# The first part of a four-layer graph network kernel in another order: own rows' sums and U ahead, two scalings on ScalarE

## The chip, the cores and the metric

The kernel runs on one core of a Trainium2 chip. The metric is the device time of one execution in microseconds (us); lower is better. The engines are TensorE (PE; its weight loads are PEld), VectorE (DVE), ScalarE (ACT), GpSimd (POOL) and SyncE (SP, which here only issues DMAs). Each runs its own list of instructions in order, and semaphores tie the lists together.

## The reference, cut to what matters

Sixteen graphs of 512 nodes with 128 features go through four layers, each followed by a layer norm:

```python
x = _layernorm(x + _L0_gnn_ref(x, adj, ...))   # adj @ (x @ W) + bias
x = _layernorm(x + _L1_gnn_ref(x, adj, ...))   # 5 groups of the first 25 nodes, two graph convolutions each
x = _layernorm(x + _L2_gnn_ref(x, adj, ...))   # mask * exp(e_i + f_j), rows normalised, times h
x = _layernorm(x + _L3_gnn_ref(x, adj, ...))   # conv 17 taps, gaussian message passing, GRU cell
```

Layer 1 touches the first 25 nodes of a graph alone. For each group it takes the block of the adjacency that the group's mask leaves, adds the identity, and scales it on both sides by the inverse root of its row sums:

```python
A = adj + jnp.eye(n)
deg = jnp.sum(A, axis=-1)
norm_adj = dinv[:, :, None] * A * dinv[:, None, :]     # dinv = deg ** -0.5
support = jnp.einsum('bnd,de->bne', x, W)
out = jax.nn.relu(jnp.einsum('bnm,bme->bne', norm_adj, support) + b)
```

## The kernel before

The program has two parts with a barrier of all engines between them. The second part is a software pipeline over the sixteen graphs. It starts at 72.83 us, and the change leaves it as it is. The first part prepares all that the pipeline needs: graph 0 through layers 0 to 2, layer 1 of the other fifteen graphs at once, and the weights.

The fifteen graphs are packed as `PT` = 3 tiles of `PJ` = 5 graphs with 25 nodes each, so `R` = 125 rows. What the first part does for them, by the names in the code:

- `mask_blocks(t)` (DVE) makes the masked blocks `A5[t]` of 5 groups and their row sums `deg`. `inverse_degrees` turns the sums into inverse roots with a power that POOL computes (`degree_root`). The blocks are scaled by rows (L730), `block_rows(t)` (PE) transposes them into PSUM, and `scale_columns(t)` (DVE, L596) scales the other side into `nadjT`.
- `own_sums(q)` (PE, L888) computes layer 0 for the first 25 nodes of each graph ("own rows"), four graphs at a time. It needs the x tiles `xt[0..2]`, which SP loads one after the other. ACT copies the sums (`copy_natural`), PE transposes them (`transpose_sums`), ACT copies them again (`copy_sums`), and `own_outputs` (L903) multiplies by the weight. DVE adds x (L791), takes statistics (L795, L799) and normalises (L810) to `x1P`; the semaphore is `q_nP`.
- The products U = `x1P` times `nadjT` (L1056, L1057) follow, then `hidden(gi)`, `second_layer(gi)` and `mix_nodes(gi)` for the five groups. Between them stand `transpose_second(mc)`, which turns the adjacency of graph 1, and `transpose_weights(k)`, which turns the weights of layer 3. ACT rounds the turned weights (`round_weights`), DVE keeps the rest (`rest_of_weights`).

Beside that runs graph 0: its hidden products (L993), second layer (L1009) and mix (L1015), DVE's masked outputs (L747), their sum (L752), statistics, x2, a dot product that gives `ef` (L632), ACT's exponential `pef` (L528), and the split of x2 times `pef` into `x_hi` (ACT, L531) and `x_lo` (DVE, L787). The second aggregate (L264 to L266: twelve passes of 512 columns into bank 5) uses them, and `OUT2` (L1048) is the product of that aggregate with layer 2's weight.

The order of each engine is written out by hand, and the PSUM banks are given by hand too (`W_BANK`, `TT_BANK`). SP's list waits at two places: the load of the 17 taps (`nat_c2`, L383) waits for `own_sums(1)`, since it overwrites `xt[0]`, and the load of the adjacency of graph 1 is behind it.

## Time and profile before

| | us |
| --- | --- |
| median of 3 runs | 576.24 |
| lowest, highest | 575.03, 576.47 |
| the profiled execution, its device time | 576.53 |
| the profiled execution, its span | 574.8 |
| PE busy | 552.4 |
| DVE busy | 481.9 |
| ACT busy | 393.2 |
| POOL busy | 218.1 |

Times in the trace count from the start of the span. A timeline row gives the start, the length, the engine, the line, the operation with its operands, how many instructions were merged (x), and in brackets how long the engine stood idle just before and what released it. One fp32 product on PE appears as two matmuls in the trace, so x10 there is five in the code. A merged row's length runs from the start of its first to the end of its last instruction.

### The profile page before, as it was taken

To read this page: it belongs to the slowest core of one execution; us is meant where nothing else is said; L and a number is where in the kernel's file an instruction comes from. 1 tells how busy PE (TensorE), PEld (TensorE's weight loads), DVE (VectorE), ACT (ScalarE), POOL (GpSimd) and SP (SyncE) were. 2 spreads that over 40 slices of the span, in tenths; PEclk is the share of its full clock that TensorE was granted. 3 is DMA by queue.
4 is the path that set the end of the run, shared out by engine and by line. 5 is a ranking of instruction groups with operands and counts; after the bars stand their busy time and mean duration, and the time that the engine had idled before them with its cause. 6 is when DMAs were issued, how large, how long until landed. Compare 5 with 4: busy or idle time off the path is not lost.

```text
span 574.8 us, 12128 instructions
## 1 busy us (share of the span) xinstructions
PE 552.4 (96%) x3639; PEld 487.4 (85%) x3639; DVE 481.9 (84%) x1768; ACT 393.2 (68%) x828; POOL 218.1 (38%) x213
## 2 busy tenths in 40 slices
PE   5879999999999999999999999999999999999994
PEld 5767988888989898989889898989898888989684
DVE  3897868889898988888888989888888889898665
ACT  2425666777786867777678778687677777786452
POOL 3311134353444435263534435353525353443010
PEclk9998999999999999999999999999999999999998
DMA  7890041003030303020020303030302103000000
GB/s 183 261 328 13 2 133 68 2 14 100 1 111 0 110 0 110 0 88 23 24 86 0 110 0 110 0 110 0 110 0 58 52 10 101 2 19 19 1 21 18
DMA packets 33301, 34.46 MB, mean 60 GB/s; under 512 B 1663, under 2 KB 22531, under 8 KB 33146
## 3 DMA queue, kind: packets, MB, share of 16 engines
q1 hardware_dynamic: 32986, 34.01, 18.7%
q8 instruction: 13, 0.21, 0.2%
q10 hardware_dynamic: 288, 0.13, 0.1%
q14 instruction: 14, 0.11, 0.1%
HBM read 29.74 MB, written 4.39 MB: 59 GB/s over the span
## 4 chain that ended last, share of the span: by engine, by line
PE 85%; DVE 1%; ACT 1%; issue 0%; POOLq 0%; POOL 0%; DVEq 0%
PE bank L264 14%; PE bank L266 14%; PE bank L265 14%; PE pair L264 6%; PE pair L266 6%; PE pair L265 6%; PE bank L1665 5%; PE bank L1676 3%; PE bank L1769 2%; PE pair L1825 2%; PE pair L1757 2%; PE bank L1860 2%; PE bank L1861 2%; PE bank L1864 2%; PE bank L1730 1%; PE bank L1840 1%
## 5 line engine op out<-in xcount | busy, mean ns | idle before, releaser
L1153 POOL TENSOR_TENSOR rs<-ve,neg_half 128x4 f32<-128x4 f32 (+1 forms) x60 | 54.8, 913 | 134.9 <-DVE ve L1389 100.9
L1187 POOL TENSOR_TENSOR P_lo<-P,P_hi 128x512 fp32r<-128x512 f32 x56 | 81.9, 1482 | 50.7 <-ACT P_hi L1226 50.7
L264 PE MATMUL bank<-cd_hi,w_hi 128*128 128x256 f32 x272 | 77.1, 284 | 0.0
L265 PE MATMUL bank<-cd_lo,w_hi 128*128 128x256 f32 x272 | 76.5, 281 | 0.0
L266 PE MATMUL bank<-cd_hi,w_lo 128*128 128x256 f32 x272 | 76.2, 280 | 0.0
L1424 DVE TENSOR_TENSOR P<-bank,aT 128x512 f32<-128x512 f32 x64 | 41.1, 684 | 18.5 <-ACT bank L1212 18.4
L264 PE MATMUL pair<-aT_hi,x_hi 128*128 128x512 f32 x128 | 53.3, 416 | 1.4 <-DVE x_lo L787 1.4
L265 PEld LDWEIGHTS bank<-cd_lo,w_hi 128*128 128x128 f32 x272 | 51.2, 188 | 1.6
L264 PEld LDWEIGHTS bank<-cd_hi,w_hi 128*128 128x128 f32 x272 | 51.3, 189 | 1.4
L266 PEld LDWEIGHTS bank<-cd_hi,w_lo 128*128 128x128 f32 x272 | 51.4, 189 | 0.0
L266 PE MATMUL pair<-aT_hi,x_lo 128*128 128x512 f32 x128 | 51.0, 398 | 0.0
L265 PE MATMUL pair<-aT_lo,x_hi 128*128 128x512 f32 x128 | 50.7, 396 | 0.0
L1226 ACT ACTIVATE P_hi<-P 128x512 fp32r<-128x512 f32 x56 | 32.2, 630 | 17.9 <-DVE P L1424 17.9
L1408 DVE TENSOR_TENSOR aT_lo<-bank,aT_hi 128x512 fp32r<-128x512 f32 x56 | 38.5, 687 | 6.9 <-ACT aT L1208 6.9
L1163 POOL TENSOR_TENSOR x<-x_nat,bias 128x512 f32<-128x512 f32 x15 | 19.7, 1314 | 64.1 <-DVE x3T_lo L1494 64.1
L264 PE MATMUL bank<-co_hi,w_hi 128*128 128x256 f32 x144 | 41.8, 290 | 0.2 <-DVE co_lo L1511 0.2
L266 PE MATMUL bank<-co_hi,w_lo 128*128 128x256 f32 x144 | 40.7, 282 | 0.0
L265 PE MATMUL bank<-co_lo,w_hi 128*128 128x256 f32 x144 | 40.5, 281 | 0.0
L1208 ACT ACTIVATE aT<-bank 128x512 f32<-128x512 f32 x56 | 34.8, 621 | 0.0
L1212 ACT ACTIVATE bank<-bank 128x512 f32<-128x512 f32 x64 | 34.4, 575 | 0.0
L1206 ACT ACTIVATE aT_hi<-bank 128x512 fp32r<-128x512 f32 x56 | 34.3, 613 | 0.0
L1345 ACT ACTIVATE nmp_hi<-bank 128x512 fp32r<-128x512 f32 x16 | 9.6, 600 | 35.8 <-PE bank L1864 32.2
(378 smaller groups left out, 1696.1 us busy)
## 6 DMA issues: line engine op xcount, KB each, us to landing
adj_nat<-in_adj_dram SPq DMA_DIRECT2D x16, 1024.0 KB, 5.9
x_nat<-in_x_dram SPq DMA_DIRECT2D x16, 256.0 KB, 2.9
xt<-in_x_dram SPq DMA_DIRECT2D x3, 1280.0 KB, 11.1
out_dram<-y_out SPq DMA_DIRECT2D x15, 256.0 KB, 2.3
hw<-in_L_gnn_W_dram SPq DMA_DIRECT2D x2, 640.0 KB, 6.5
xt<-in_L_gnn_conv_w_dram SPq DMA_DIRECT2D x1, 1088.0 KB, 6.9
aT<-in_adj_dram SPq DMA_DIRECT2D x5, 96.0 KB
nat_ih<-in_L_gnn_w_ih_dram SPq DMA_DIRECT2D x1, 384.0 KB, 5.7
```

Of the source, the lines that this page charges most:

```text
L264: nc.tensor.matmul(o, lh, rh, start=start, stop=False)
L265: nc.tensor.matmul(o, lh, rl, start=False, stop=False)
L266: return nc.tensor.matmul(o, ll, rh, start=False, stop=stop)
L1153: g.tensor_tensor(rs[i][:, 0:n], ve[i][:, 0:n], neg_half[:, 0:n], ALU.pow).then_inc(po_rs[i], 1)
L1187: g.tensor_tensor(P_lo[:, mc, :], P[:, mc, :], f(P_hi[:, mc, :]), ALU.subtract).then_inc(po_Plo[mc], 1)
L1206: s.activation(aT_hi[:, mc, :], AT_OF[mc][:, :], ACT.Identity)
L1208: s.activation(aT[par][:, mc, :], AT_OF[mc][:, :], ACT.Identity).then_inc(ac_aT[mc], 1)
L1212: s.activation(AT_BANK[mc % 2][:, :], AT_BANK[mc % 2][:, :], ACT.Exp, scale=2.0).then_inc(ac_E[mc], 1)
L1226: s.activation(P_hi[:, mc, :], P[:, mc, :], ACT.Identity).then_inc(ac_Phi[mc], 1)
L1408: v.tensor_tensor(aT_lo[:, mc, :], AT_OF[mc][:, :], f(aT_hi[:, mc, :]), ALU.subtract).then_inc(dv_aTlo[mc], 1)
L1424: v.tensor_tensor(P[:, mc, :], AT_BANK[mc % 2][:, :], aT[par][:, mc, :], ALU.mult).then_inc(dv_P[mc], 1)
L1665: last = t_.transpose(AT_OF[mc][:, ch(c)], adj_nat[par][:, c, ch(mc)], ident[:, :])
```

## The change

The work stays the same, apart from three moves between engines or banks; the rest is order.

- The scaling of the masked blocks by rows (L730, three DVE instructions of 125x625) becomes `scale_rows(t)`: five ACT instructions of 125x125 for each tile. DVE's `inverse_degrees` for it moves ahead of `c12`.
- The scaling of the 17 taps (L842, one DVE instruction of 128x2176) becomes one ACT instruction in `scale_taps`, ahead of ACT's copy of the second aggregate.
- `transpose_sums` writes bank 5 in place of bank 0, and two weight groups change banks.
- On PE `block_rows(1)` goes ahead of graph 0's mix, the sums of all own rows go ahead of the blocks of tiles 2 and 3, `transpose_sums` goes ahead of the first weights, `transpose_weights(1)` and the products U go ahead of `OUT2`, and `transpose_second(0)` goes behind `hidden(0)`.
- On DVE `scale_columns` of tiles 1 and 2 goes behind graph 0's statistics, the sum and the statistics of the own rows go ahead of the split `x_lo`, and the rests of two weight groups move.
- On POOL the sum of tap pairs goes ahead of graph 0's last inverse root and waits for `dv_e`.

SP's list is unchanged. The diff, cut:

```diff
-        W_BANK = [bank[i] for i in (4, 4, 1, 6, 5, 0, 1, 6, 5, 0)]
-        NAT_BANK, TT_BANK = bank[4], bank[0]
+        W_BANK = [bank[i] for i in (4, 6, 0, 6, 5, 0, 1, 6, 5, 0)]
+        NAT_BANK, TT_BANK = bank[4], bank[5]
...
+                def scale_rows(t):
+                    for gi in range(NG):
+                        last = s.activation(A5[0:R, t, gi, :], A5[0:R, t, gi, :], ACT.Identity,
+                                            scale=deg[0:R, 3, NG * t + gi:NG * t + gi + 1])
+                    last.then_inc(q_B, 1)
...
+                act.wait_ge(q_dgi, 2)
+                scale_rows(1)
                 act.wait_ge(q_S0, 1)
...
+                scale_rows(2)
+                scale_rows(3)
                 copy_natural()
+                copy_sums()
                 round_weights(-1)
-                copy_sums()
...
+                round_weights(0)
+                round_weights(1)
+                scale_taps()
+                act.wait_ge(pe_agg2, 1)
+                s.activation(agg_sb[:, :], AG_BANK[:, :], ACT.Identity).then_inc(ac_agg2, 1)
                 for t in range(PT):
                     copy_u(t)
+                act.wait_ge(dv_e, 1)
+                s.activation(pef[:, 0, :], ef[:, 0, :], ACT.Exp, bias=c12[:, 0:1]).then_inc(ac_pe, 1)
+                relu_hidden(0)
                 split_second(0)
-                relu_hidden(0)
                 split_second(1)
...
                 v.tensor_scalar(hT0[:, :, :], hT0[:, :, :], 0.0, None, ALU.max).then_inc(q_own, 2)
+                inverse_degrees(R, NG, NT * NG, 2)
                 dve.wait_ge(q_vsb, 1)
...
-                inverse_degrees(R, NG, NT * NG, 2)
-                for t in range(1, NT):
-                    v.tensor_tensor(A5[0:R, t], A5[0:R, t], spread(deg[0:R, 3, NG * t:NG * (t + 1)], R), ALU.mult).then_inc(q_B, 1)
...
-                v.tensor_scalar(nat_c2, nat_c2, bn_scale[:, 1:2], None, ALU.mult).then_inc(q_sc2, 1)
...
+                block_rows(1)
                 pe.wait_ge(q_c12, 1)
                 pe.wait_ge(q_S0s, 1)
...
-                block_rows(1)
                 own_sums(1)
-                block_rows(2)
-                block_rows(3)
                 own_sums(2)
                 own_sums(3)
+                block_rows(2)
                 pe.wait_ge(q_sumsb, 1)
+                transpose_sums()
                 pe.wait_ge(q_sc1, 1)
                 transpose_weights(-1)
-                transpose_sums()
+                block_rows(3)
...
+                pe.wait_ge(q_whi, 1)
                 pe.wait_ge(q_nP, 5)
                 pe.wait_ge(q_nT, NT + 1)
                 for t in range(PT):
...
+                pe.wait_ge(ac_agg2, 1)
+                pe.wait_ge(q_unit, 1)
+                pe.wait_ge(q_wlo, 1)
+                for c in range(NC):
+                    last = t_.matmul(OUT2[:, c // 2, c % 2, :], agg_sb[:, ch(c)], wwT, start=True, stop=True)
+                last.then_inc(pe_out2, 1)
                 hidden(0)
+                pe.wait_ge(adj_in[1], 16)
                 pe.wait_ge(q_wlo, 2)
+                transpose_second(0)
                 transpose_second(1)
```

DVE at the degrees and the row scaling; hT is graph 0's hidden layer, c its two constants, hb the second bias. Before:

```order
L709 TENSOR_SCALAR hT<-hT 128x250
L711 COPY c<-bank 128x2
...
L724 TENSOR_REDUCE hsum<-hb 125x128
L727 TENSOR_TENSOR fused_in<-x,hsum 25x128
L577 TENSOR_TENSOR deg<-deg 125x15
L730 TENSOR_TENSOR A<-A,deg 125x625 x3
L632 ISA prod,ef<-x,v 128x128
```

And now:

```order
L725 TENSOR_SCALAR hT<-hT 128x250
L593 TENSOR_TENSOR deg<-deg 125x15
L728 COPY c<-bank 128x2
...
L741 TENSOR_REDUCE hsum<-hb 125x128
L744 TENSOR_TENSOR fused_in<-x,hsum 25x128
L648 ISA prod,ef<-x,v 128x128
```

The inverse degrees (deg 125x15) come eight rows earlier, behind hT, and the three scalings of 125x625 are gone; the products for `ef` (ISA rows) follow `fused_in` directly.

DVE ahead of the second aggregate; bank in L791 (now L798) is the own rows' product. Before:

```order
L747 SCALAR_TENSOR_TENSOR prod<-pair,wm,hb 25x128
L596 TENSOR_TENSOR nadjT<-bank,deg 125x500
L752 TENSOR_REDUCE red<-prod 25x128
...
L777 TENSOR_SCALAR x<-x,mv,rs 128x128
L632 ISA prod,ef<-x,v 128x128
L632 ISA ef 128x1
L782 CAST x_hi<-pef 128x4
L784 TENSOR_TENSOR x_lo<-pef,x_hi 128x4
L787 SCALAR_TENSOR_TENSOR x_lo<-x,pef,x_hi 128x127 x4
L791 TENSOR_TENSOR x1P<-bank,xP 125x384
```

And now:

```order
L761 SCALAR_TENSOR_TENSOR prod<-pair,wm,hb 25x128
L765 TENSOR_REDUCE red<-prod 25x128
...
L775 TENSOR_SCALAR ve<-mv 128x1
L612 TENSOR_TENSOR nadjT<-bank,deg 125x500 x2
...
L648 ISA prod,ef<-x,v 128x128
L648 ISA ef 128x1
L798 TENSOR_TENSOR x1P<-bank,xP 125x384
L802 BN_STATS stP<-x1P 125x6 x3
L805 CAST x_hi<-pef 128x4
L807 TENSOR_TENSOR x_lo<-pef,x_hi 128x4
L810 SCALAR_TENSOR_TENSOR x_lo<-x,pef,x_hi 128x127 x4
```

One scaled tile of columns no longer stands ahead of the sum `red`, two stand behind the statistics, and the own rows' sum and statistics stand ahead of the cast and the split `x_lo`.

PE from the last passes of the second aggregate to the second layer. Before:

```order
L266 MATMUL pair<-aT_hi,x_lo 128x512
L946 MATMUL bank<-ident,adj_nat 128x128 x4
L1048 MATMUL pair<-plainT,agg_sb 128x130 x4
L939 MATMUL bank<-ident,nat_ih 128x128 x4
L1056 MATMUL bank<-nadjT,x1P 128x125
L1057 MATMUL bank<-nadjT,x1P 128x300
...
L916 MATMUL bank<-A,hw 128x375 x2
L946 MATMUL bank<-ident,adj_nat 128x128 x4
L925 MATMUL bank<-hw,aPT 125x128 x6
```

And now:

```order
L266 MATMUL pair<-aT_hi,x_lo 128x512
L1056 MATMUL bank<-nadjT,x1P 128x125
L1057 MATMUL bank<-nadjT,x1P 128x300
...
L1064 MATMUL pair<-plainT,agg_sb 128x130 x4
L925 MATMUL bank<-A,hw 128x375 x2
L955 MATMUL bank<-ident,adj_nat 128x128 x8
L934 MATMUL bank<-hw,aPT 125x128 x6
```

U (nadjT, x1P) follows the aggregate directly, `OUT2` (plainT, agg_sb) comes behind it, and all eight transposes of graph 1's adjacency stand behind the hidden products.

## Rows read from the trace of the kernel before

**Rows 1.** Stretches of the span: us, busy by engine (instructions), PEclk, DMA share, GB/s

```profile
38.00:43.00 5.00, 2.49 (x18) 2.11 (x19) 3.81 (x20) 2.82 (x11) 1.15 (x2) 0.96 0.98 359
43.00:48.00 5.00, 4.75 (x17) 3.57 (x17) 4.69 (x16) 1.16 (x3) 0.85 (x1) 0.70 0.10 36
...
73.00:574.00 501.00, 493.54 (x3144) 435.36 (x3142) 427.84 (x1558) 362.38 (x760) 201.96 (x179) 1.00 0.14 46
```

**Rows 2.** Timeline, DVE, 28 to 48 us: start, us, engine, line, operation [idle before]

```profile
28.27 0.16 DVE L711 COPY c<-bank 128x2 f32<-128x2 f32 x1
...
31.75 2.25 DVE L730 TENSOR_TENSOR A<-A,deg 125x625 f32<-125x625 f32 x3
...
35.27 1.11 DVE L747 SCALAR_TENSOR_TENSOR prod<-bank,wm,hb 25x128 f32<-25x128 f32 x4
...
36.56 0.66 DVE L596 TENSOR_TENSOR nadjT<-bank,deg 125x500 f32<-125x500 f32 x1
...
41.08 0.29 DVE L632 CUSTOM_DVE_ANT_0 prod<-x,v 128x128 f32<-128x128 f32 x1
...
42.31 1.23 DVE L787 SCALAR_TENSOR_TENSOR x_lo<-x,pef,x_hi 128x127 fp32r<-128x127 f32 x4
43.45 0.55 DVE L791 TENSOR_TENSOR x1P<-bank,xP 125x384 f32<-125x384 f32 x1
44.11 0.68 DVE L795 BATCH_NORM_STATS2 stP<-x1P 125x6 f32<-125x128 f32 x3
...
47.61 0.85 DVE L810 TENSOR_SCALAR x1P<-x1P,mvP,rsP 125x128 f32<-125x128 f32 x3
```

**Rows 3.** Timeline, POOL, first 74 us

```profile
26.25 2.76 POOL L423 TENSOR_TENSOR deg<-deg,neg_half 125x15 f32<-125x15 f32 x1 [2.76 <-DVE deg L571]
...
37.60 0.99 POOL L432 TENSOR_TENSOR xP<-xP,bias 125x384 f32<-125x384 f32 x1 [7.93 <-DMA xP<-in_x_dram]
...
59.28 1.90 POOL L441 TENSOR_TENSOR xt<-xt 128x1024 f32<-128x1024 f32 x1 [2.56 <-DVE xt L842]
```

**Rows 4.** Timeline, ACT, first 74 us

```profile
21.37 1.57 ACT L512 ACTIVATE aT<-bank 128x512 f32<-128x512 f32 x3
...
41.81 1.27 ACT L531 ACTIVATE x_hi<-x,pef 128x127 fp32r<-128x127 f32 x4
```

**Rows 5.** Timeline, PE, 31 to 73 us

```profile
31.57 1.03 PE L1015 MATMUL bank<-prod,nadjT 25*25 25x128 f32 x8 [0.93 <-ACT prod L523]
...
35.78 1.95 PE L888 MATMUL bank<-xt,aPT 128*32 128x128 f32 x56
...
42.81 0.77 PE L264 MATMUL pair<-aT_hi,x_hi 128*128 128x512 f32 x1 [1.36 <-DVE x_lo L787]
...
46.90 0.39 PE L266 MATMUL pair<-aT_hi,x_lo 128*128 128x512 f32 x1
...
49.41 0.38 PE L1056 MATMUL bank<-nadjT,x1P 125*128 125x125 f32 x2
...
54.73 1.55 PE L925 MATMUL bank<-hw,aPT 128*125 128x128 f32 x12 [0.32 <-ACT aPT L475]
...
57.03 0.82 PE L934 MATMUL bank<-S,nadjT 125*125 125x128 f32 x6
...
72.83 0.63 PE L1730 MATMUL bank<-ident,x 128*128 128x128 f32 x4 [1.25 <-PEq L1086]
```

**Rows 6.** Loads of the x tiles, by tile: count, shortest/median/longest issue ns, first and last start

```profile
L350 SPq DMA_DIRECT2D xt<-in_x_dram x3: 389/889/4240, 11.6 to 21.3; - x3
```

**Rows 7.** DMA issues: the x tile issued last, in its own stretch; then the taps' load

```profile
xt<-in_x_dram SPq DMA_DIRECT2D x1, 1280.0 KB, 14.1
...
xt<-in_L_gnn_conv_w_dram SPq DMA_DIRECT2D x1, 1088.0 KB, 6.9
```

**Rows 8.** Timeline, DVE, 57 to 62 us

```profile
57.86 1.34 DVE L842 TENSOR_SCALAR xt<-xt,bn_scale 128x2176 f32<-128x2176 f32 x1
...
60.36 1.23 DVE L612 TENSOR_TENSOR fusedP<-R,hsum 125x384 f32<-125x384 f32 x1
```

More of the change, by code:

```diff
@@ L436, in _ @@
                 g.tensor_tensor(rsP[0:R, :], veP[0:R, :], neg_half[0:R, 0:PT], ALU.pow).then_inc(q_rsP, 1)
-                pool.wait_ge(dv_ve[2], 1)
-                g.tensor_tensor(rs[2][:, :], ve[2][:, :], neg_half[:, 0:NC], ALU.pow).then_inc(po_rs[2], 1)
+                pool.wait_ge(dv_e, 1)
                 pool.wait_ge(q_sc2, 1)
@@ L441, in _ @@
                 g.tensor_tensor(nat_sum, nat_c2[:, :, 0:TAPS - 1:2], nat_c2[:, :, 1:TAPS:2], ALU.add).then_inc(q_sum, 1)
+                pool.wait_ge(dv_ve[2], 1)
+                g.tensor_tensor(rs[2][:, :], ve[2][:, :], neg_half[:, 0:NC], ALU.pow).then_inc(po_rs[2], 1)
             @block.scalar
@@ L531, in _, with scale_taps @@
                     s.activation(x_hi[:, c, 1:D], x2[:, c, 1:D], ACT.Identity, scale=pef[:, 1, c:c + 1]).then_inc(ac_xs[c], 1)
-                round_weights(0)
-                act.wait_ge(pe_agg2, 1)
-                s.activation(agg_sb[:, :], AG_BANK[:, :], ACT.Identity).then_inc(ac_agg2, 1)
-                act.wait_ge(dv_e, 1)
-                s.activation(pef[:, 0, :], ef[:, 0, :], ACT.Exp, bias=c12[:, 0:1]).then_inc(ac_pe, 1)
-                round_weights(1)
+                def scale_taps():
+                    act.wait_ge(q_bns, 2)
+                    act.wait_ge(q_wc2, 16)
+                    s.activation(nat_c2, nat_c2, ACT.Identity, scale=bn_scale[:, 1:2]).then_inc(q_sc2, 1)
                 def split_second(mc):
@@ L749, in _ @@
                 last.then_inc(q_own, 1)
-                scale_columns(1)
                 dve.wait_ge(q_own, 5)
@@ L762, in _ @@
                 v.tensor_scalar(ve[1][:, 0:1], mv[1][:, 0, 1:2], EPS, None, ALU.add).then_inc(dv_ve[1], 1)
+                scale_columns(1)
+                scale_columns(2)
                 dve.wait_ge(q_bnr, 1)
@@ L780, in _ @@
                 dot(1, 0).then_inc(dv_f, 1)
+                dve.wait_ge(q_o, 1)
+                dve.wait_ge(q_xPb, 1)
+                v.tensor_tensor(x1P[0:R, :, :], bank[7][0:R, 0:PT * D].rearrange("p (t d) -> p t d", t=PT), xP[0:R, :, :],
+                                ALU.add).then_inc(q_nP, 1)
+                hold(dve, q_nP, 1)
+                for t in range(PT):
+                    last = v.bn_stats(stP[0:R, t, :], x1P[0:R, t, :])
+                last.then_inc(q_nP, 1)
                 hold(dve, ac_pf, 1)
@@ L788, in _ @@
                                            ALU.mult, ALU.subtract).then_inc(dv_xs[c], 1)
-                dve.wait_ge(q_o, 1)
-                dve.wait_ge(q_xPb, 1)
-                v.tensor_tensor(x1P[0:R, :, :], bank[7][0:R, 0:PT * D].rearrange("p (t d) -> p t d", t=PT), xP[0:R, :, :],
-                                ALU.add).then_inc(q_nP, 1)
-                hold(dve, q_nP, 1)
-                for t in range(PT):
-                    last = v.bn_stats(stP[0:R, t, :], x1P[0:R, t, :])
-                last.then_inc(q_nP, 1)
                 hold(dve, q_nP, 2)
@@ L802, in _ @@
                 v.tensor_scalar(veP[0:R, :], mvP[0:R, :, 1], EPS, None, ALU.add).then_inc(q_nP, 1)
-                scale_columns(2)
                 scale_columns(3)
@@ L815, in _ @@
                 last.then_inc(dv_e, 1)
+                rest_of_weights(0)
+                rest_of_weights(1)
                 hold(dve, pe_out2, 1)
@@ L828, in _ @@
                 last.then_inc(dv_y3, 1)
-                rest_of_weights(1)
                 rest_of_second(0)
@@ L1034, in _ @@
                 transpose_weights(0)
+                pe.wait_ge(q_nT, 2)
+                transpose_weights(1)
                 pe.wait_ge(dv_pf, 1)
@@ L1041, in _ @@
                 last.then_inc(pe_agg2, 1)
-                pe.wait_ge(adj_in[1], 16)
-                pe.wait_ge(q_TTs, 1)
-                transpose_second(0)
-                pe.wait_ge(ac_agg2, 1)
-                pe.wait_ge(q_unit, 1)
-                for c in range(NC):
-                    last = t_.matmul(OUT2[:, c // 2, c % 2, :], agg_sb[:, ch(c)], wwT, start=True, stop=True)
-                last.then_inc(pe_out2, 1)
-                pe.wait_ge(q_nT, 3)
-                transpose_weights(1)
-                pe.wait_ge(q_wlo, 1)
+                pe.wait_ge(q_whi, 1)
                 pe.wait_ge(q_nP, 5)
```

6 lines of the change are left out of this document (removed).

## The prediction

> **What bounds the kernel now.** I read the stretches first, then each engine's timeline of the first 73 us. Behind 73 us PE is busy 493.54 of 501 us at full clock [rows 1], and the change leaves that code alone. So the question is when the second part starts; it does at 72.83 us [rows 5]. Before that PE is busy 2.49 of the 5 us from 38 to 43 [rows 1]. There it waits for a chain over DVE, POOL and ACT: graph 0's outputs, sum, statistics and `ef`, then the split `x_lo`, which the second aggregate waits for until 42.81 [rows 5]. PE's granted clock fell behind that thin stretch: it is 0.70 in the mean of 43 to 48 us [rows 1], which is 3.0 us at the lower level (1.2 GHz) and the rest at 2.4 GHz. The U products wait for PE's own order until 49.41 [rows 5]. From the second layer on (54.73) PE runs nearly without gaps to the barrier. Below, steps of 0.65 us or less without a group are the small instructions and hand-overs of the same timelines, moved with their own lengths.
>
> **Step 1, the degrees, a wait added on DVE.** POOL's power ends at 29.01 [rows 3]. `inverse_degrees` used to come long after it; now DVE reaches it at 28.2, since its next row starts at 28.27 [rows 2]. DVE waits some 0.8 us, and with the operation itself and its hand-over `c12` starts at 29.25, 0.98 late. All of DVE is queued behind. In return the three scalings (31.75, 2.25 us) and the old place of the degrees leave, 33.92 - 31.57 = 2.35 us. Graph 0's outputs (L747) start at 35.27 + 0.98 - 2.35 = 33.90, 1.37 earlier.
>
> **Step 2, the scalings on ACT.** Four scaled activations of 127 columns take 1.27 us [rows 4], 0.3 us from start to start, so five take 1.6: 29.25 to 30.8. ACT's copy of graph 0's S0 waits behind them; PE's second layer ended at 30.64 (31.57 less the 0.93 idle [rows 5]), so the copy loses some 0.1. `block_rows(1)` fits into the wait that stood there, and the mix starts at about 31.55 as before and ends near 32.7, which is ahead of DVE at 33.90: no cost. Tiles 2 and 3 take 3 us on ACT, 31.4 to 34.4, ahead of a copy that isn't due before 37.4: no cost, by the cover of the loads.
>
> The Trainium skill's page "ScalarE: Activation LUTs" (What ACT_TABLE_LOAD costs) gives 280 ns and 0.833 ns a column for an activation with a pointer operand. By it the scaled 125 columns take 0.38 us, and the trace agrees (its x_hi rows are 0.38 to 0.40 long, 1.27 for four that overlap); the taps of 2176 columns would take 2.1 us by that estimate, and the sum below would not change.
>
> **Step 3, the own rows' sums.** The third x tile is issued at 21.3 [rows 6] and lands 14.1 us later [rows 7], at 35.4. PE reaches the sums that need it at about 33.75 and waits 1.7 us. The sums used to start at 35.78 and last 1.95 [rows 5], so they end at 37.4, only 0.35 earlier: the loads hold this branch. Then `block_rows(2)` (0.65) covers ACT's copy, the transposed sums, first weights and `block_rows(3)` cover the second copy, and `own_outputs` ends at 40.3.
>
> **Step 4, graph 0's statistics.** The sum of the outputs no longer has `scale_columns(1)` ahead of it (0.58 of the 0.66 in the row is its own step [rows 2]), so the statistics are 1.37 + 0.58 = 1.95 earlier, at 37.65. Two scalings of columns (1.17) follow, so the bn rows, x2 and the dot product come 0.78 earlier: 41.08 becomes 40.30 [rows 2]. POOL's inverse root stands behind the x sum that ends at 38.59 [rows 3]; with 0.56 it is done at 39.2, under DVE's scalings.
>
> **Step 5, the own rows ahead of the split.** DVE now does the sum and the statistics (0.55 and 0.68 [rows 2], 1.27 with the hand-over) between the dot product and the cast, where 0.43 us of waiting for ACT stood. That eats the 0.78: the cast comes at 41.87, `x_lo` starts at 42.37 for 42.31 before, and the aggregate at 42.87 for 42.81. The term is zero, from -0.8 (were it hidden) to +0.8 (were `own_outputs` late by that much).
>
> **Step 6, the clock.** Where PE was thin before, it now has all its transposes and weights: busy from 35.45 to 41.2 almost without a gap, idle 33.75 to 35.45 and 41.2 to 42.87. I take it that the clock stays up. The twelve passes took 42.81 to 46.90 from first to last start [rows 5]; 3.0 us at the lower level are 1.5 at the upper, so it is 2.6 now. The aggregate ends at 45.8 instead of 47.2. The range is 0 to 1.5.
>
> **Step 7, U.** DVE still needs after `x_lo` (1.2): aggregation and variance (0.5), one scaling of columns (0.6) and the last (0.46), then, with POOL's root under them, the normalisation (0.85 [rows 2]): 43.5 to 46.0. Before, 1.23 of sum and statistics, one more scaling and a weights' rest stood between as well. U starts at 46.1 for 49.41, 3.3 earlier, bound by DVE and no longer by PE. ACT's taps scaling (between the DVE's 1.34 [rows 8] and, by four times the width of a 0.49 us copy [rows 4], 2.1) runs 43.3 to 45.4, ahead of the copy of the aggregate due at 45.9: hidden, by 0.5 us; if it is late, `OUT2` is, behind U's 2.2 us of cover.
>
> **Step 8, to the second layer.** U ends at 48.3, `OUT2` (1.0) at 49.3, `hidden(0)` (1.3) at 50.6, eight transposes (0.9) at 51.5. Beside them `y3` is done at 51.4 and the relu at 51.4. The second layer starts at 51.5 for 54.73: 3.2 earlier. Now ACT is late: two split pairs and x_hi, five copies of 0.5 [rows 4], run 51.4 to 53.9 ahead of `copy_s2(0)`. So the first `mix_nodes` starts at 54.4 for 57.03 [rows 5], 2.6 earlier; 0.5 is given back.
>
> **Step 9, the tail.** From there PE has the same list as before and I let it keep its pace. DVE is later against PE than before, by up to 1 us, but has lost the taps (1.34). On POOL the tap pairs leave the tail. There `fusedP` (60.36) took 1.23 us while POOL's 1.90 us sum ran [rows 3, 8]. The Trainium skill's page "SBUF — State Buffer" (Who interferes with whom) says that a DVE instruction with two SBUF inputs contends with a GpSimd instruction that reads SBUF. By that rule and this row the tail loses a stall of some 0.6 on DVE. At the new place DVE's weight rests read one operand from PSUM, and by the same rule they don't stall. Without it the rivals below hold as they are, with a thinner margin.
>
> **The sum.** Against the profiled execution (span 574.8, device time 576.53): -2.6 at the barrier, plus 0.2 that I add for new hand-overs between engines, is -2.4, so 574.1. That execution lies 0.3 over the median of the three runs (576.24), for which I forecast 573.8.
>
> **The rivals.**
> A, the clock falls again. PE has 1.7 us of idle twice, the second just ahead of the aggregate; for the fall speaks that before it fell behind 2.5 busy us in 5, against it that PE is now busy some six in nine. Then the aggregate ends at 47.2 and U starts there: 1.1 less gain, 574.9.
> B, the tail becomes DVE's and ACT's. The third mix needs DVE's second group added by 61.9 and my replay has it at 61.85; if DVE's chain from the late `aT_lo` (52.4 for 53.40, only 1.0 earlier) sets the end, the gain is between 1.0 and 1.6: 575.0. Against it, PE is ahead of DVE's need by 0.6 or more at all later places.
> C, slower: the x rows of POOL's sum land later. That wait ended at 37.60 [rows 3], and the taps' load (1088 KB, 6.9 us [rows 7]) is issued 0.8 earlier, since `own_sums(1)` ends earlier. At 359 GB/s [rows 1] it is 3.0 us of traffic. If it goes ahead of those rows, POOL's sum ends at 41.6, the root at 42.2, the dot at 42.8, and with step 5's 1.3 in front the aggregate starts at 45.3 at the lower clock, U at 49.65, the first mix at 57.9 for 57.03: 577.1, and 578 with one more half us at any wait. It turns into a loss when the rows land more than 2.3 us late. Against it: they were issued before the taps.
> D, more gain: ACT's backlog of step 8 is hidden and no hand-over costs: -3.2, 573.0.
>
> **How the numbers follow.** Forecast 0.54, A 0.2, B 0.13, C 0.06, D 0.07. The bound of what a measurement tells apart is 0.3%, 1.7 us: faster means below 574.5. The forecast is faster in nine cases of ten, D always, A and B in one of five: 0.62. C gives slower in two of three: 0.04. The rest, 0.34, is the same. The range goes from 572.8 (D) to 575.8 (A or B with 0.8 to spare).
>
> **What would show it.** The first steps: DVE idle 0.8 ahead of the degrees, L761 (graph 0's outputs) near 33.9, PE idle until 35.4 ahead of the sums. Then the cast near 41.9, the aggregate's passes at 0.39 and not 0.77, U at 46.1, the second layer at 51.5, the first mix with 0.5 of wait for ACT, and the second part's first row (72.83 before) at 70.4. Passes at 0.77 mean A; idle on PE ahead of L943 behind the first mix means B; POOL's sum later than 37.6 means C.

## The result, and the profile after

| | before | changed |
| --- | --- | --- |
| median, us | 575.19 | 574.25 |
| lowest to highest | 573.91 to 578.61 | 572.86 to 575.77 |
| runs | 19 | 19 |
| the profiled execution, device time | 576.53 | 573.76 |
| its span | 574.8 | 572.0 |

The ratio is 0.9969, 95% interval 0.9954 to 0.9983: the change takes 0.31% off, 0.9 us at the medians, where the forecast took off 2.4. The two profiled executions lie 2.8 us apart. Most of this text is about that difference.

PE's timeline of the changed kernel, 32 to 70 us, answers [rows 5]:

```profile
32.53 1.08 PE L898 MATMUL bank<-xt,aPT 128*32 128x128 f32 x32
35.05 1.95 PE L898 MATMUL bank<-xt,aPT 128*32 128x128 f32 x56 [1.44 <-DMA xt<-in_x_dram]
...
42.35 0.47 PE L264 MATMUL pair<-aT_hi,x_hi 128*128 128x512 f32 x1 [1.42 <-DVE x_lo L810]
...
44.94 0.39 PE L266 MATMUL pair<-aT_hi,x_lo 128*128 128x512 f32 x1
45.87 0.46 PE L1056 MATMUL bank<-nadjT,x1P 125*128 125x125 f32 x2 [0.54 <-issue]
...
51.35 1.58 PE L934 MATMUL bank<-hw,aPT 128*125 128x128 f32 x12
...
54.02 0.92 PE L943 MATMUL bank<-S,nadjT 125*125 125x128 f32 x6 [0.17 <-ACT S L490]
...
69.92 0.63 PE L1738 MATMUL bank<-ident,x 128*128 128x128 f32 x4 [1.25 <-PEq L1094]
```

The aggregate starts 0.46 us earlier than in [rows 5], and its twelve passes take 2.59 us from first to last start, where they took 4.09. U starts 0.93 behind the start of the last pass. The second part starts at 69.92 for 72.83, and from there to the end it is 502.1 us for 502.0: nothing changed behind the barrier.

The stretches of the changed kernel, for the first two of [rows 1]:

```profile
38.00:43.00 5.00, 3.58 (x29) 3.25 (x29) 4.62 (x23) 3.27 (x11) 0.63 (x2) 1.00 0.88 308
43.00:48.00 5.00, 4.46 (x23) 3.38 (x22) 4.33 (x19) 3.57 (x5) 2.16 (x2) 1.00 0.08 31
```

PE is busy 3.58 of the 5 us ahead of the aggregate, and the granted clock is 1.00 in both stretches.

DVE of the changed kernel, 28 to 46 us, answers [rows 2]:

```profile
28.77 0.17 DVE L593 TENSOR_TENSOR deg<-deg 125x15 f32<-125x15 f32 x1 [0.91 <-POOL deg L423]
...
33.60 1.11 DVE L761 SCALAR_TENSOR_TENSOR prod<-bank,wm,hb 25x128 f32<-25x128 f32 x4
...
40.12 0.29 DVE L648 CUSTOM_DVE_ANT_0 prod<-x,v 128x128 f32<-128x128 f32 x1
40.34 0.08 DVE L648 DVE_READ_ACCUMULATOR2_ANT ef<- 128x1 f32 x1
40.34 0.55 DVE L798 TENSOR_TENSOR x1P<-bank,xP 125x384 f32<-125x384 f32 x1
40.99 0.68 DVE L802 BATCH_NORM_STATS2 stP<-x1P 125x6 f32<-125x128 f32 x3
41.59 0.15 DVE L805 CAST x_hi<-pef 128x4 fp32r<-128x4 f32 x1
...
44.90 0.86 DVE L823 TENSOR_SCALAR x1P<-x1P,mvP,rsP 125x128 f32<-125x128 f32 x3 [0.38 <-issue]
```

DVE waits 0.91 us for the degrees, and the own rows' sum and statistics stand between the dot product and the cast without a gap. The scaled `x1P`, which U needs, is 2.71 us earlier than in [rows 2].

ACT and then DVE's tail of the changed kernel; they answer [rows 4] and [rows 8]:

```profile
28.98 1.56 ACT L468 ACTIVATE A<-A,deg 125x125 f32<-125x125 f32 x5 [1.09 <-DVE deg L593]
...
42.98 2.11 ACT L546 ACTIVATE xt<-xt,bn_scale 128x2176 f32<-128x2176 f32 x1
45.36 0.60 ACT L556 ACTIVATE agg_sb<-pair 128x512 f32<-128x512 f32 x1 [0.28 <-PE pair L266]
```

```profile
57.84 0.56 DVE L628 TENSOR_TENSOR fusedP<-R,hsum 125x384 f32<-125x384 f32 x1
```

### The profile page after: what moved, and what is told of

The parts are those of the page before. It is cut to its first block, busy times and chain, and to the rows that moved or that the text cites. A ratio compares the mean times of both kernels' runs of the same rounds, so it can differ in the third digit from the quotient of the medians.

```text
span 572.0 us, 12140 instructions
## 1 busy us (share of the span) xinstructions
PE 552.4 (97%) x3639; PEld 488.0 (85%) x3639; DVE 479.0 (84%) x1764; ACT 398.9 (70%) x844; POOL 218.7 (38%) x213
## 4 chain that ended last, share of the span: by engine, by line
PE 85%; DVE 1%; ACT 1%; issue 0%; POOLq 0%; POOL 0%; DVEq 0%
PE bank L264 14%; PE bank L266 14%; PE bank L265 14%; PE pair L264 6%; PE pair L266 6%; PE pair L265 6%; PE bank L1673 5%; PE bank L1684 3%; PE bank L1777 2%; PE pair L1833 2%; PE pair L1765 2%; PE bank L1868 2%; PE bank L1869 2%; PE bank L1872 2%; PE bank L1738 1%; PE bank L1848 1%
## 5 line engine op out<-in xcount | busy, mean ns | idle before, releaser
L266 PEld LDWEIGHTS bank<-cd_hi,w_lo 128*128 128x128 f32 x272 | 51.5, 189 | 0.0
```

Of the source, the lines that this page charges most:

```text
L266: return nc.tensor.matmul(o, ll, rh, start=False, stop=stop)
```

## The experiments

The runs are told in the order of the questions. In the tables, "clock low" is where the granted clock of a trace stood at its lower level (1.2 GHz) in the first 73 us, from stretches of 1 us; elsewhere it was 2.4 GHz. "Adjacency" is the start of PE's transposes of graph 0's adjacency (L968, before L959), which wait for its load.

### Is the first trace typical? Both kernels again

**The changed kernel, unchanged.**

> The changed kernel unchanged, timed beside the kernel before on the same chip, for its spread. Its trace starts the second part 2.9 us earlier (69.92 for 72.83), yet the medians of 19 runs each differ by 0.9 us. Theory 1 (the clock varies by execution): the fall ahead of the second aggregate happens in some executions of either kernel, so the mean granted clock differs from run to run and goes with the time; ratio to before 0.996 to 0.998. Theory 2 (the order alone): every execution gains the 2.6 to 2.9 us of the traces; ratio 0.9950 to 0.9955.

Measured: 574.5 us, ratio 0.9976 (0.996 to 0.9992). Its profiled execution took 576.44, as long as the one of before. PE in it:

```profile
44.42 0.77 PE L264 MATMUL pair<-aT_hi,x_hi 128*128 128x512 f32 x1 [1.42 <-DVE x_lo L810]
44.98 0.63 PE L265 MATMUL pair<-aT_lo,x_hi 128*128 128x512 f32 x1
...
48.66 0.38 PE L1056 MATMUL bank<-nadjT,x1P 125*128 125x125 f32 x2
```

The passes are 0.63 long: the clock is low in the aggregate of the changed kernel too, with the same instructions and the same 1.42 us of wait ahead of it as in the first trace. So the clock that stayed up in the first trace does not belong to its program.

**The kernel before, twice more**, and the changed kernel a third time.

> The kernel before, unchanged, for a second trace of it. Theory (the clock falls at places that differ from one execution to the next): the granted clock is at its lower level somewhere else than at 42.6 to 46 us; if it stays up through the aggregate, the aggregate's passes take 0.39 us each, OUT2 follows 1.4 us earlier than 47.98, and the second part starts at 71.0 to 71.8 instead of 72.83, counted from the same landing of the adjacency (11.6). Rival (the fall in the aggregate belongs to this program): low at 42 to 46 again, the aggregate's passes 0.63 us, the second part at 72.5 to 73.2. Both: 501.9 to 502.1 us from the start of the second part to the end.

> The kernel before, unchanged, for a third trace of it, to see what its stretch from the aggregate to the second part takes where the clock is up in the aggregate: in both traces so far the clock is low there (30.02 and 30.13 us), in the kernel before with idle transposes it is up (28.55, with U held by nothing of DVE's). Theory (about 1.0 to 1.5 us of the distance between the two first traces is this fall, which comes in some executions only): if the rows show the clock up from 42 to 47 us, 28.5 to 29.1 from the aggregate's start to the second part's, so that against the changed kernel's 27.57 there are 1.0 to 1.5 left, as the medians say; if it is low there again, 29.9 to 30.2, and the question is left to the medians. Rival (the kernel before is slow there for another reason, DVE's order): 29.5 or more with the clock up.

> The changed kernel, unchanged, for a third trace. Theory: the low stretches are at other places again; between the adjacency's landing and U there are 34.5 us where the clock stays up in between (34.55 in the first trace of it) and 37 to 37.6 where a stretch lies in the first layer as well as in the aggregate (37.6 in the second trace). The start of the second part is 24.0 to 24.1 us behind U in either case. Rival (the first trace is what this kernel does, the second was a disturbance): 34.5 us again and the lower level at 11.8 to 15.1 alone.

Measured, one execution each: 577.9, 573.86 and 574.79 us. Of the second of these, the kernel before with its granted clock up throughout, this is PE; the last rows are 40 to 70 us:

```profile
19.38 0.48 PE L980 MATMUL bank<-ident,vrows 28*128 28x128 f32 x2 [1.23 <-DMA vrows<-in_L_gnn_b_dram]
...
40.92 0.47 PE L264 MATMUL pair<-aT_hi,x_hi 128*128 128x512 f32 x1 [1.33 <-DVE x_lo L787]
...
43.49 0.39 PE L266 MATMUL pair<-aT_hi,x_lo 128*128 128x512 f32 x1
...
45.57 0.60 PE L939 MATMUL bank<-ident,nat_ih 128*128 128x128 f32 x4
46.67 0.46 PE L1056 MATMUL bank<-nadjT,x1P 125*128 125x125 f32 x2 [0.50 <-issue]
...
52.06 1.55 PE L925 MATMUL bank<-hw,aPT 128*125 128x128 f32 x12 [0.32 <-ACT aPT L475]
...
54.37 0.82 PE L934 MATMUL bank<-S,nadjT 125*125 125x128 f32 x6
...
70.17 0.63 PE L1730 MATMUL bank<-ident,x 128*128 128x128 f32 x4 [1.25 <-PEq L1086]
```

The stretches of the same execution:

```profile
38.00:43.00 5.00, 3.41 (x19) 2.92 (x20) 3.99 (x20) 2.16 (x7) 0.42 (x1) 1.00 0.71 252
43.00:48.00 5.00, 4.25 (x28) 3.37 (x28) 4.46 (x20) 1.15 (x3) 0.85 (x1) 1.00 0.01 2
```

All traces of the two kernels, and one of the changed kernel with its degrees later (below), in us:

| kernel | clock low | adjacency | to the aggregate | from there to U | from the aggregate to the second part | adjacency to second part |
| --- | --- | --- | --- | --- | --- | --- |
| before, first | 12 to 15, 42 to 46 | 11.61 | 31.20 | 6.60 | 30.02 | 61.22 |
| before, second | 20 to 31, 44 to 48 | 10.58 | 33.58 | 6.71 | 30.13 | 63.71 |
| before, third | nowhere | 10.09 | 30.83 | 5.75 | 29.25 | 60.08 |
| changed, first | 12 to 15 | 11.32 | 31.03 | 3.52 | 27.57 | 58.60 |
| changed, second | 20 to 31, 44 to 48 | 11.04 | 33.38 | 4.24 | 28.23 | 61.61 |
| changed, third | 20 to 28 | 10.99 | 32.06 | 3.51 | 27.57 | 59.63 |
| degrees later | nowhere | 11.51 | 31.07 | 3.51 | 27.57 | 58.64 |

Like with like, counted from the adjacency: with the clock up everywhere the changed order is worth 60.08 - 58.64 = 1.4 us; with the low stretches at the same two places (the two second traces) 2.1; in the first pair, where only before's aggregate was slow, 2.6. The second trace of before had its aggregate slow again, so it spoke for the rival there; the third decides it, since the same program ran its aggregate at 0.39 us a pass. Its 29.25 lies between what was expected, 28.5 to 29.1, and the 29.5 or more of the rival that named DVE's order, and both have a part in it: with the clock up U waits until DVE's `x1P` is ready (46.57; it starts at 46.67). The third trace of the changed kernel has a low stretch at a third place, ahead of the aggregate only, and U comes 35.6 us behind the adjacency, between the two figures that were expected; the second part follows U by 24.06. The clock is not all of that: graph 0's outputs start where they did in the first trace (33.62 for 33.60), and what then comes late is the third x tile (36.02 for 35.05), behind which PE turns the blocks that DVE waits for. Two other sources of spread are as large as the effect: a trace with a low stretch at 20 to 31 us is 2.3 us (33.38 for 31.07, changed order) to 2.8 (33.58 for 30.83, before) longer up to the aggregate, and the adjacency lands anywhere from 10.1 to 11.6.

The 1.4 us has a weak part and a firm one. Ahead of the aggregate PE waits for loads that don't follow the adjacency at a fixed distance: 1.23 us for `vrows` in the third trace of before (above), 0.47 in the run with the degrees later. Counted from the start of the trace, the second parts of these two start at the same time, 70.17 and 70.15. Behind the aggregate no load is waited for, and there every trace of the changed kernel is ahead of every trace of before, by 1.68 us where the clock is up in both (29.25 and 27.57) and by 1.9 where it is low in both (30.13 and 28.23).

Over all timed runs, single executions left out, the kernel before takes 575.70 in the mean of 104 runs (spread 1.3), the changed one 574.42 in 31 (spread 0.9): 1.3 us less, 95% interval 0.9 to 1.7 from these spreads. By the clock, where it is on record: the runs whose mean granted clock over the span is 0.995 or more have means of 574.4 (before, 17 runs) and 573.6 (changed, 8); those from 0.987 to under 0.991, 576.6 (25) and 574.7 (11). By these means the change is worth 0.7 us where the clock hardly fell and 1.9 where it did.

### Can idle products hold the clock up?

```diff
+                def keep_busy(n):
+                    for i in range(n):
+                        t_.transpose(bank[5][:, 0:D], ident[:, :], ident[:, :])
...
+                keep_busy(11)
```

In the changed kernel `keep_busy(11)` stands ahead of `own_sums(2)` and ahead of the aggregate. The second kernel is the kernel before with 5, 4 and 11 of them in its three gaps.

> The changed kernel with eleven idle transposes of the identity into bank 5 in each of PE's two gaps (ahead of the sums that wait for the third x tile, and ahead of the second aggregate). They add no work that anyone waits for. If the clock falls in these gaps in some executions (theory 1), the median drops by up to 0.5 us and the spread shrinks. If it never falls there (theory 2), the time is that of the changed kernel within 0.2 us.

> The kernel before with idle transposes into bank 5 in its three gaps between 37.7 and 42.8 us (five, four and eleven). If the fall of the clock cost it time (theory 1), the second aggregate's passes are 0.39 us long and no longer 0.77, the aggregate ends 1.4 us earlier, and U starts at 48.5 for 49.41, since DVE's normalisation ends only then: 0.9 us less at the start of the second part, and up to 0.9 in the median. If the clock was not what held U (theory 2: DVE's chain did), the time is that of before within 0.2.

Measured: 574.08 us, ratio 0.9971 (0.9953 to 0.9989), no different from the changed kernel; and 576.41, ratio 1.0012 (0.9992 to 1.0032), no faster than before. In both profiled executions the aggregate ran at the upper level, but low stretches stood elsewhere (12 to 15 and 26 to 29 us in the one, 20 to 27 and 34 to 37 in the other). That says little, since the clock was up in the aggregate of three of the six traces without idle products too. In the kernel before the idle products also stood in the aggregate's way:

```profile
43.14 1.36 PE L951 MATMUL pair<-ident 128*128 128x128 f32 x11
44.26 0.48 PE L264 MATMUL pair<-aT_hi,x_hi 128*128 128x512 f32 x1
```

The aggregate starts without any wait, so `x_lo` was ready while they ran: its split had started at 42.62, and in [rows 2] and [rows 5] the aggregate follows the start of the split by 0.50, where here it is 1.64. Filling the gaps in this way brings nothing; a filling that costs no wait was not tried on the kernel before.

### The scalings on ACT

The changed kernel with the row scaling back on DVE behind `fused_in`, and the degrees with it:

```diff
-                act.wait_ge(q_dgi, 2)
-                scale_rows(1)
...
-                scale_rows(2)
-                scale_rows(3)
...
-                inverse_degrees(R, NG, NT * NG, 2)
...
+                inverse_degrees(R, NG, NT * NG, 2)
+                for t in range(1, NT):
+                    v.tensor_tensor(A5[0:R, t], A5[0:R, t], spread(deg[0:R, 3, NG * t:NG * (t + 1)], R), ALU.mult).then_inc(q_B, 1)
```

> The changed kernel with one part undone: the masked blocks are scaled by rows on DVE again, in three instructions behind fused_in, with the degrees there too, and ACT doesn't scale them. By steps 1 and 2 of the prediction DVE's chain gets 1.37 us longer, so graph 0's outputs are 1.37 later, the split x_lo at 43.2, and since U is bound by DVE it starts 1.4 later; the second part starts 1.2 to 1.4 later and the time is 1.2 to 1.4 over that of the changed kernel. Rival: the loads and the transposed sums (the own rows' branch) hold the chain, then the loss is under 0.5.

Measured: 575.35 us, ratio 0.9995 (0.9973 to 1.0016). PE and DVE in it:

```profile
32.28 0.81 PE L884 MATMUL bank<-ident,A 125*125 125x125 f32 x5 [1.94 <-DVE A L742]
```

```profile
31.41 2.25 DVE L742 TENSOR_TENSOR A<-A,deg 125x625 f32<-125x625 f32 x3
...
34.92 1.10 DVE L759 SCALAR_TENSOR_TENSOR prod<-bank,wm,hb 25x128 f32<-25x128 f32 x4
```

Graph 0's outputs start at 34.92 for 33.60, the aggregate at 43.73 for 42.35, U at 46.87 for 45.87, the second part at 70.93 for 69.92. This trace has low stretches at 20 to 24 and 34 to 38 us, and its adjacency landed 1.5 earlier; but graph 0's hidden layer starts on DVE when it does in the changed kernel (27.07 for 27.04), and from there to `x1P` DVE stands idle for nothing, so the rows can be compared. Graph 0's outputs are 1.3 late, as expected; U is 1.0 late, since 0.38 us in which DVE stood idle ahead of the last scaling of `x1P` is gone. By the trace ACT's scaling is worth 1.0 us; by the medians 0.85 (575.35 for 574.5, measured together), which lies within their intervals. Without it no gain over before can be measured.

### The own rows ahead of the split

The changed kernel with the sum and the statistics of the own rows moved back behind `x_lo` (L810), nothing else; these lines leave their place ahead of the cast and stand behind the split:

```diff
-                dve.wait_ge(q_o, 1)
-                dve.wait_ge(q_xPb, 1)
-                v.tensor_tensor(x1P[0:R, :, :], bank[7][0:R, 0:PT * D].rearrange("p (t d) -> p t d", t=PT), xP[0:R, :, :],
-                                ALU.add).then_inc(q_nP, 1)
-                hold(dve, q_nP, 1)
-                for t in range(PT):
-                    last = v.bn_stats(stP[0:R, t, :], x1P[0:R, t, :])
-                last.then_inc(q_nP, 1)
```

> The changed kernel with the own rows' sum and statistics behind the split x_lo again, as before the change. Step 5 of the prediction: the split starts 1.27 us earlier (41.1 in the trace's time), the aggregate starts and ends 1.2 earlier, but DVE has the same work ahead of x1P, so U does not move (45.9) and the time is that of the changed kernel within 0.3. Rival: the aggregate is what holds U when the granted clock falls there, then this kernel is faster by up to 0.6 in the median.

Measured: 576.64 us, ratio 1.0014 (0.9996 to 1.0033): this move alone gives the whole gain back. Measured together with it, the run with the degrees later (below), which keeps the changed kernel's order here, took 574.29. DVE in it:

```profile
40.55 0.08 DVE L648 DVE_READ_ACCUMULATOR2_ANT ef<- 128x1 f32 x1
41.07 0.17 DVE L797 CAST x_hi<-pef 128x4 fp32r<-128x4 f32 x1 [0.43 <-ACT pef L539]
...
42.71 0.55 DVE L806 TENSOR_TENSOR x1P<-bank,xP 125x384 f32<-125x384 f32 x1
...
46.15 0.86 DVE L823 TENSOR_SCALAR x1P<-x1P,mvP,rsP 125x128 f32<-125x128 f32 x3 [0.38 <-issue]
```

And PE:

```profile
42.07 0.47 PE L264 MATMUL pair<-aT_hi,x_hi 128*128 128x512 f32 x1 [0.92 <-DVE x_lo L802]
...
47.11 0.46 PE L1056 MATMUL bank<-nadjT,x1P 125*128 125x125 f32 x2 [2.04 <-DVE x1P L823]
```

The split comes 0.52 earlier (41.07 for 41.59) and the aggregate 0.28, but the sum stands 2.37 later and U waits 2.04 for it. U, and the second part with it, is 1.25 late (47.11 and 71.17 for 45.87 and 69.92). Of these differences 0.21 us was there before the order differs: `ef` is read at 40.55 for 40.34. So the order costs the aggregate 0.5 and is worth 1.0 to U.

I had expected no difference for U, since DVE has the same work ahead of `x1P` in either order. It has, but not the same gaps: from the reading of `ef` to the scaling of `x1P` it takes 5.60 us for 4.56. With the own rows first, their sum fills the half microsecond in which DVE otherwise waits for `pef`. The other half is won in small steps, where an instruction no longer stands right behind the one whose result it needs: the split starts 0.08 behind the row before it for 0.29, and the statistics' aggregation, 0.78 behind the statistics here, has the split in between.

The trace shows 1.0 us, the medians over 2. The rest isn't shown, but one thing bears on it. The run of three moves (below) has the same order and the same wait of 2.04 ahead of U, and in its trace the clock is low right behind, from 47 to 51 us, so that the way from U to the second layer takes 7.11 for 5.48. The twelve runs with the split first have a mean granted clock of 0.989, those of the changed kernel 0.992 and 0.993. By my estimate a further low stretch of 3.5 us in each run would take 3.5 / 2 / 575 = 0.003 off that mean.

### U's place alone

The kernel before with nothing but U moved ahead of `OUT2` on PE, and its copies on ACT with it:

```diff
+                for t in range(PT):
+                    copy_u(t)
...
-                for t in range(PT):
-                    copy_u(t)
...
+                pe.wait_ge(q_wlo, 1)
+                pe.wait_ge(q_nP, 5)
+                pe.wait_ge(q_nT, NT + 1)
+                for t in range(PT):
+                    t_.matmul(bank[2 + t][:, 0:R], x1P[0:R, t, :], nadjT[0:R, t + 1, 0, :], start=True, stop=True)
```

> The kernel before with one part of the change alone: PE issues the products U right behind the second aggregate, ahead of the transposes, OUT2 and weights, and ACT copies U there. DVE's normalisation ended at 48.46 in the trace of before and U started at 49.41. Theory (order alone gives little, DVE's chain holds U): U starts at 48.5, and OUT2 with y3 come 1.5 later, so the second layer is 0.2 to 0.7 earlier and the time is within 0.7 of before. Rival (PE's order held U and everything behind it): 0.9 less or more.

Measured: 579.32 us, ratio 1.0053 (1.003 to 1.0077): slower than before. PE, 48 to 58 us:

```profile
48.55 0.46 PE L1046 MATMUL bank<-nadjT,x1P 125*128 125x125 f32 x2 [2.77 <-DVE x1P L810]
...
52.52 1.49 PE L1056 MATMUL pair<-plainT,agg_sb 128*128 128x130 f32 x8
...
57.20 1.47 PE L925 MATMUL bank<-hw,aPT 128*125 128x128 f32 x12
```

And DVE behind it:

```profile
54.18 0.16 DVE L818 TENSOR_TENSOR dq<-pair,pef 128x4 f32<-128x4 f32 x1 [4.89 <-PE pair L1056]
```

U starts 0.86 earlier than in [rows 5], but that is the clock, which is up in this aggregate: from the start of the aggregate to U it is 5.76 us, and 5.75 in the third trace of before, with `OUT2` ahead. DVE's `x1P` sets U in both. So nothing is gained; PE stands 2.77 for U, and `OUT2`, which used to fill that time, comes at 52.52; the normaliser of graph 0 waits 4.89 for it, and the second layer starts at 57.20 for 54.73. Low stretches of the clock (32 to 37 and 50 to 54 us) are in this trace too, so its size is not all the order's; the medians carry the verdict. The early U is worth something only where DVE's `x1P` is ahead.

### Smaller moves on the changed kernel

The inverse degrees ahead of `hb2` in place of ahead of `c12`:

```diff
-                inverse_degrees(R, NG, NT * NG, 2)
                 dve.wait_ge(q_vsb, 1)
...
+                inverse_degrees(R, NG, NT * NG, 2)
```

> The changed kernel with the inverse degrees five small DVE instructions later, ahead of the bias scaling, so that DVE no longer waits 0.91 us for POOL's power. Graph 0's outputs start 0.8 earlier, the dot product too, but the own rows' sum waits for own_outputs (39.95 at best for 40.34), so the split and U come 0.3 to 0.4 earlier; time 0.3 to 0.4 below the changed kernel. Rival: ACT's scaling of tile 1, which starts 0.4 later then, holds graph 0's mix; then no gain.

Measured: 574.29 us, ratio 0.9985 (0.9968 to 1.0003). DVE no longer waits for POOL, and stands ahead of graph 0's outputs instead; PE is held by the third x tile as before:

```profile
27.76 0.17 DVE L593 TENSOR_TENSOR deg<-deg 125x15 f32<-125x15 f32 x1
...
32.84 1.11 DVE L761 SCALAR_TENSOR_TENSOR prod<-bank,wm,hb 25x128 f32<-25x128 f32 x4 [1.09 <-issue]
```

```profile
35.56 1.95 PE L898 MATMUL bank<-xt,aPT 128*32 128x128 f32 x56 [1.81 <-DMA xt<-in_x_dram]
```

The 0.3 to 0.4 us that I expected don't come. DVE's lead ends at the second scaling of columns:

```profile
38.28 0.68 DVE L612 TENSOR_TENSOR nadjT<-bank,deg 125x500 f32<-125x500 f32 x1 [0.97 <-PE bank L886]
```

It needs `block_rows(2)`, which stands on PE behind the sums that the third x tile holds. So the wait of step 1 is real and costs nothing: from the adjacency to the aggregate it is 31.07 for 31.03.

The same with the split first (the order of the run above) and ACT's `x_hi` of graph 1 behind the first group's copies:

> The changed kernel with three moves: the degrees later (no wait for POOL), the own rows' sum and statistics behind the split, and ACT's rounding of graph 1's x behind its copies for the first group. The aggregate ends 1.5 earlier, U starts 0.8 earlier (DVE's chain less the wait), the first mix no longer waits for ACT (0.2 to 0.4). Time 0.8 to 1.2 below the changed kernel, some 0.5% below the kernel before. Rival: the loads (third x tile at 35.0) hold the own rows' branch; then under 0.4.

Measured: 575.59 us, ratio 1.0005 (0.9984 to 1.0026). I had expected 0.8 to 1.2 us less than the changed kernel, and it is slower. U waits 2.04 for `x1P` here as well, as in the run with that order alone. Last, without that order:

```diff
-                act.wait_ge(x_in[1], 16)
-                s.activation(x_hi[:, :, :], x_nat[1][:, :, :], ACT.Identity).then_inc(ac_xhi, 1)
...
+                    if gi == 0:
+                        act.wait_ge(x_in[1], 16)
+                        s.activation(x_hi[:, :, :], x_nat[1][:, :, :], ACT.Identity).then_inc(ac_xhi, 1)
```

> The changed kernel with two moves: its inverse degrees of the own rows are taken in front of hb2's, so that DVE waits for nothing of POOL's at 28.8 us, and ACT rounds graph 1's x_hi behind its copies of the first group of transposes instead of in front of them; own rows' sum and statistics stay ahead of the split, as in the changed kernel. Theory (with the split behind own rows' sum U comes 1.2 us earlier than with it in front, which was what made the run of three moves slow): U at 34.5 to 34.6 us behind the adjacency's landing where the clock stays up, the second part 24.0 behind U, a ratio to before of 0.996 to 0.999, no different from the changed kernel. If ACT's earlier copies shorten the chain up to U: ratio 0.994 to 0.997. Rival (ACT's later x_hi holds graph 1's aggregate, and that is what cost in the run of three moves): 24.8 or more from U to the second part, ratio 0.999 to 1.002.

Measured: 574.82 us, ratio 0.9982 (0.9958 to 1.0006). Its trace has the shortest first part of all, 58.31 from the adjacency to the second part. The first mix starts 2.33 behind the second layer's start and waits for nothing of ACT's, where the changed kernel takes 2.67 (54.02 - 51.35). Of these 0.3 us the tail gives back 0.13 (16.03 from the first mix to the second part for 15.90). The rest is not to be told from the changed kernel in the medians; I can't call it better.

## Why the prediction was right or wrong

**The changed kernel's own course was forecast well.** The adjacency lands 0.3 us earlier in its first trace than in before's; with that taken off, the steps stand as put down, within some 0.2:

| | forecast | trace |
| --- | --- | --- |
| graph 0's outputs (step 1) | 33.90 | 33.60 |
| third x tile, sums start (step 3) | 35.4 | 35.05 |
| dot product (step 4) | 40.30 | 40.12 |
| cast (step 5) | 41.87 | 41.59 |
| aggregate (step 5) | 42.87 | 42.35 |
| U (step 7) | 46.1 | 45.87 |
| second layer (step 8) | 51.5 | 51.35 |
| first mix (step 8) | 54.4 | 54.02 |
| second part | 70.4 | 69.92 |

**Steps 1 and 3** held: DVE waits 0.91 for the degrees (0.8 was put down), and the third x tile holds PE 1.44 (1.7). **Step 2** held, and its worth is shown by the run with the scalings back on DVE. By the estimate from the Trainium skill's page "ScalarE: Activation LUTs" (What ACT_TABLE_LOAD costs) the taps' 2176 columns take 2.1 us; the row says 2.11, and ACT was still in time for the aggregate's copy, by 0.28 us.

**Step 5** put the aggregate where it was, and that is right: 31.03 us behind the adjacency for 31.20. The order by itself costs the aggregate 0.5, as the run with the split first shows. But the step counted only the aggregate; for U the same order is worth 1.0. Step 7 has that gain in its sum: it takes the 1.23 of sum and statistics out of the stretch between `x_lo` and U. That moving work within one engine's list should gain anything, since the work stays the same, neither step explains; the gaps that it fills do.

**Step 6, the clock, is the term that was mis-sized.** It put 1.4 to 1.5 us of gain for the aggregate on the granted clock staying up (1.1 at U, by rival A), because one trace of before showed it low in the aggregate. In three traces of before it was low there twice, in three of the changed kernel once. So a part of the time both kernels pay it, and a part of the time neither does. And where before doesn't pay it, it doesn't gain 1.5: with the clock up its U waits for DVE (46.67, idle 0.50; `x1P` is done at 46.57) and the way from the aggregate to the second part shrinks from 30.02 to 29.25, by 0.77. With the clock low PE came to U after `x1P` was ready, so a part of the slow passes lay over a wait that PE would have had anyway. In the changed kernel the fall cost 0.66 (28.23 for 27.57), where step 6 and rival A had 1.5 and 1.1. The changed order is what differs in all executions: with the clock up, 29.25 - 27.57 = 1.68 us less behind the aggregate, of which 2.24 are won up to U (5.75 and 3.51) and 0.56 given back behind it, 0.36 of them between the second layer and the first mix. With a 0.2 loss ahead of the aggregate, which the loads blur, 1.4 are left. Rival A, the clock falls again, is not one case with a chance of 0.2 but a state that each execution of either kernel can be in. Its sign, passes at 0.77, was misread as well: 0.77 is the first pass of [rows 5], and the others took 0.63.

**Step 8** had the backlog on ACT, 0.5 us given back; it was 0.36, and moving `x_hi` took it away, for 0.13 in the tail. **Step 9**: the tail kept its pace, 15.90 us from the first mix to the second part for 15.80 in [rows 5], so rival B did not come. `fusedP` took 0.56 us, where it took 1.23 beside POOL's sum [rows 8], and no work of POOL's stands beside it now. That agrees with the rule of the page "SBUF — State Buffer" in the Trainium skill (Who interferes with whom) by which the prediction expected it, though the pace of the tail shows that the 0.6 us were worth nothing: PE sets it. At its new place (46.69, 1.89 us) POOL's sum lies beside DVE's two rests of weights, which take 0.68 each as ever.

**Rival C**, the x rows of POOL's sum landing later: the sum started at 37.12 for 37.60, so no.

**The level.** The sum said 2.4 us less; the medians say 0.9, all runs together 1.3. The forecast of 573.8 still came within 0.5 us of 574.25, and that is luck: the gain was put 1.5 us too high, and so was the base, by 1.05, since the three runs of before had a median of 576.24, where 19 have 575.19 (575.7 to 576.1 in the later measurements). The profiled execution of before, 576.53, was one with two low stretches. Both errors are of one kind: one execution, or three, taken for the kernel.

**Rival D**, more gain, can be judged now: nothing of it was left besides the 0.2 to 0.3 of ACT's backlog.

What stays open: why the granted clock falls where it falls. In these two programs it fell at 12 to 15, at 12 to 15 and 42 to 46, at 20 to 31 and 44 to 48, at 20 to 28, or nowhere. PE's idle time differs with the landing of the loads, and some of the falls go with it. In the four of all fourteen traces in which PE stood idle longest ahead of the adjacency's transposes (3.21 to 3.75 us) the clock is low from 12; of the ten others it is low there in one, the changed kernel's first. No trace has both a low stretch at 12 and one at 20. Two of the three traces in which PE waited 2 us or more ahead of U have one behind it (50 and 47 us); the run with the split first has none. So PE's waits have a part in it, and they don't settle it.

## What to carry to other kernels

A profiled execution is one draw: before a low stretch of the clock is counted as a gain to be had, look whether it stands at the same place in a second and a third trace, and what becomes late next if it goes. Price a move for every reader of what is moved; here two groups of DVE instructions put into a wait of 0.43 us cost the aggregate half a microsecond and brought U forward by a whole one. A product moved ahead on an in-order engine has to come with the work that feeds it: alone it made this kernel 0.5% slower, together with its feeders it belongs to the 0.3% gain.

## What the runs showed of the hardware

- The granted clock of one and the same program differs from one execution to the next in the first 73 us: no low stretch, one of some 3 us, one of 7, or two. At the lower level a pass of 512 columns takes 0.63 us for 0.39, and the 16 transposes of the adjacency 3.46 [before, first trace] for 1.97 [before, third]. That the latter were slow cost at most 0.4 us (adjacency to aggregate 31.20 for 30.83): with them fast, PE stood 1.23 us for a load soon after [before, third], with them slow it didn't.
- The granted clock of the trace doesn't show everything. It reads 1.00 from the start, yet the same idle transposes, 32 that wait for nothing from 3.4 us on, took 4.48 us in one trace [before, first] and 6.06 in another [changed, first]; from 6 to 7 us the one has 12 of them and the other 6.
- Between the kernel before at a mean granted clock of 0.986 (the second trace, 577.9 us) and at 0.997 (the third, 573.86) lie 4.0 us of device time, three times what the change is worth. Of these 0.5 is the adjacency's landing (10.58 and 10.09), and the rest lies between it and the second part.
- The first load on which PE waits lands between 10.1 and 11.6 us in six traces of the two kernels, with no difference in what is issued ahead of it.
- Eleven idle transposes in a gap of PE didn't keep the low stretches away: each of the two traces with them has two.
